# Values products behind the next scores, scores three units early, three output heads, last output step set apart

## The reference

```python
x = hidden_states                                # 1 x 1024 x 512, fp32
q = rope(x @ w_q); k = rope(x @ w_k); v = x @ w_v     # 32 query heads, 8 key/value heads, of 128
lq = x @ w_lq                                    # 1024 x 128
lk = rope(lq @ w_lk); lv = x @ w_lv              # 32 latent heads of 128
attn = causal_attn(q, k, v); lat = causal_attn(q, lk, lv)
x = layernorm(x + attn @ w_o + lat @ w_lo)
x = layernorm(x + top1_lora_experts(x))          # 8 experts of rank 16
```

## Time and profile before

| | |
|---|---|
| median of 3 runs | 2124.37 us (2123.72 to 2124.85) |
| the profiled execution | 2122.39 us |
| span of its profile, first to last instruction | 2120.6 us |
| busy: PE, DVE, ACT, POOL | 2026.5, 1409.2, 1044.6, 1060.2 us |
| granted TensorE clock, mean of the span | 0.994 of full speed |

### The profile page before, as it was taken

The page is one execution under the profiler, slowest core; times in us unless marked ns, Lnnn a source line. Parts: engine busy times, 40 slices in busy tenths (PEclk is TensorE's granted clock), DMA queues, the critical chain, the costliest instruction groups (busy, mean ns, idle before and its releaser), DMA issues.

```text
span 2120.6 us, 39951 instructions
## 1 busy us (share of the span) xinstructions
PE 2026.5 (96%) x12832; PEld 1824.3 (86%) x12832; DVE 1409.2 (66%) x3404; ACT 1044.6 (49%) x2461; POOL 1060.2 (50%) x873
## 2 busy tenths in 40 slices
PE   6999999999999999999999999999999999999995
PEld 5988889888898888988898898988989888898883
DVE  5757757576675757757577675767757576575766
ACT  3644626355363644626356373554626456273651
POOL 4536465364644537445364554536455364653630
PEclk9999999999999999999999999999999999999998
DMA  5010010100001000010100001010010100100001
GB/s 169 1 33 11 2 54 1 43 1 31 24 1 43 2 32 24 1 43 1 54 1 21 23 1 54 1 33 11 2 54 1 33 11 21 34 1 31 1 11 40
DMA packets 19367, 50.86 MB, mean 24 GB/s; under 512 B 5824, under 2 KB 7872, under 8 KB 19008
## 3 DMA queue, kind: packets, MB, share of 16 engines
q1 hardware_dynamic: 19136, 48.00, 6.8%
HBM read 45.89 MB, written 2.10 MB: 23 GB/s over the span
## 4 chain that ended last, share of the span: by engine, by line
PE 45%; issue 27%; POOL 24%; DVE 3%; POOLq 0%; ACT 0%; DVEq 0%; ACTq 0%
POOL probs L672 14%; PE ps L315 13%; PE ps L316 13%; PE ps L317 13%; PE ps L402 6%; POOL probs L663 4%; POOL ql_lo L667 4%; POOL pt_lo L648 1%; DVE pt_lo L679 1%; DVE stats L804 0%; POOLq L671 0%; PE ps L495 0%; PE ps L510 0%; POOL wlk_lo L654 0%; DVE probs L715 0%
## 5 line engine op out<-in xcount | busy, mean ns | idle before, releaser
L672 POOL TENSOR_TENSOR probs<-probs,inv_sum 128x640 f32<-128x640 f32 (+7 forms) x512 | 586.3, 1147 | 493.8 <-DVE inv_sum L746 493.1
L679 DVE TENSOR_TENSOR pt_lo<-ps,pt_hi 128x512 fp32r<-128x512 f32 (+3 forms) x768 | 401.6, 551 | 202.8 <-ACT pt_hi L517 199.6
L549 ACT ACTIVATE probs<-probs,neg_max 128x640 f32<-128x640 f32 (+7 forms) x512 | 397.6, 777 | 163.5 <-DVE neg_max L739 163.5
L517 ACT ACTIVATE pt_hi<-ps 128x512 fp32r<-128x512 f32 (+3 forms) x768 | 347.1, 486 | 185.3 <-PE ps L402 171.9
L739 DVE CUSTOM_DVE_ANT_0 probs<-ps,mask 128x640 f32<-128x640 f32 (+7 forms) x512 | 384.1, 753 | 57.6 <-PE ps L317 37.2
L315 PE MATMUL ps<-pt_hi,val_hi 128*128 128x256 f32 (+1 forms) x1280 | 371.0, 290 | 31.2 <-DVE pt_lo L679 31.2
L316 PE MATMUL ps<-pt_lo,val_hi 128*128 128x256 f32 (+1 forms) x1280 | 359.7, 281 | 0.0
L317 PE MATMUL ps<-pt_hi,val_lo 128*128 128x256 f32 (+1 forms) x1280 | 358.8, 280 | 0.0
L402 PE MATMUL ps<-ident,probs 128*128 128x128 f32 x2304 | 337.2, 274 | 15.4 <-POOL probs L672 13.3
L402 PEld LDWEIGHTS ps<-ident,probs 128*128 128x128 f32 x2304 | 266.1, 140 | 49.8 <-POOL probs L672 18.7
L315 PEld LDWEIGHTS ps<-pt_hi,val_hi 128*128 128x128 f32 x1280 | 242.5, 189 | 56.5 <-issue 55.0
(11 more groups left out here) (107 smaller groups left out, 4214.7 us busy)
## 6 DMA issues: line engine op xcount, KB each, us to landing
raw<-wo SPq DMA_DIRECT2D x32, 512.0 KB, 3.3
raw<-wq SPq DMA_DIRECT2D x16, 512.0 KB, 3.3
raw<-wlv SPq DMA_DIRECT2D x16, 512.0 KB, 3.9
raw<-wkv SPq DMA_DIRECT2D x8, 512.0 KB, 3.5
acc<-xT SPq DMA_DIRECT2D x4, 512.0 KB, 5.9
acc<-x SPq DMA_DIRECT2D x1, 2048.0 KB, 7.6
wlk_raw<-wlk SPq DMA_DIRECT2D x16, 128.0 KB, 4.0
out<-acc SPq DMA_DIRECT2D x8, 256.0 KB, 2.4
```

What stands on the lines that cost most here:

```text
L517: return nc.scalar.activation(dst, src, ACT.Copy)
L549: nc.scalar.activation(dst, dst, ACT.Exp, bias=neg_max[:, n % 8:n % 8 + 1], scale=-1.0, accum_out=row_sum[:, n % 8:n % 8 + 1]).then_inc(q[ ...
L672: nc.gpsimd.tensor_tensor(b, b, inv_sum[:, k % 8:k % 8 + 1].to_broadcast([P, b.shape[-1]]), ALU.mult).then_inc(q["normed"], 1)
L679: return nc.vector.tensor_tensor(dst, src, h, ALU.subtract)
```

## The change

Four edits, all of order; no operation is added or removed.

1. `UNITS`: q(1,0), q(1,1), lk(1,0) now follow one another, and v units that stood between them come later; the list ends with five v units, with v 2 and v 3 around lk(1,1).
2. `EARLY_UNIT = 3`: scores 0 and 1, their maxima and exponentials stand one unit earlier, before the last unit but two. Scores 2, and the reciprocals of 0 and 1, stay at the last unit.
3. The products of n = 2, 10, 18, 26 are no longer cut: the whole product stands behind the scores of slot n + 5. The product of n = 30 is also whole, in slot 35.
4. Outputs: the head of y = 2 moves from slot 34 to slot 33, ahead of turn_probs(30). Steps 0 and 1 of y = 0 and of y = 1 are done first, then step 3 of both, then y = 2, then the rest as before. The head's wait on the output weights is written in another place, for the same part.

```diff
--- before.py
+++ after.py
@@ -44,6 +44,7 @@
 O_BANKS = (6, 7)
 R_LAG = 3
 EARLY, MID = 2, 1
+EARLY_UNIT = 3
 T_LAG = 3
 LO_LAG = T_LAG + 1
 PV_LONG, PV_SHORT = 1, 3
@@ -64,14 +65,14 @@
 OUT_PARTS = (("ob", 0, 512, 1536), ("oa", 0, 1024, 0), ("ob", 512, 512, 1024))
 OUT_AFTER = (CHUNKS - 5, CHUNKS - 3, CHUNKS - 1)
 
-STEP_WEIGHTS = ((2, 0), (2, 512), (2, 1536), (3, 1024))
+STEP_WEIGHTS = ((2, 0), (2, 512), (1, 1536), (3, 1024))
 
 
 UNITS = (
-    [("q", 0, 0), ("q", 0, 1), ("k", 0, 0), ("k", 0, 1), ("lk", 0, 0), ("v", 0), ("lk", 0, 1), ("v", 1), ("q", 1, 0), ("v", 2),
-     ("q", 1, 1), ("v", 3), ("lk", 1, 0), ("v", 4), ("lk", 1, 1), ("v", 5), ("v", 6), ("v", 7)],
-    [("q", 0, 0), ("q", 0, 1), ("lk", 0, 0), ("v", 0), ("lk", 0, 1), ("v", 1), ("q", 1, 0), ("v", 2),
-     ("q", 1, 1), ("v", 3), ("lk", 1, 0), ("v", 4), ("lk", 1, 1), ("v", 5), ("v", 6), ("v", 7)],
+    [("q", 0, 0), ("q", 0, 1), ("k", 0, 0), ("k", 0, 1), ("lk", 0, 0), ("v", 0), ("lk", 0, 1), ("v", 1), ("q", 1, 0),
+     ("q", 1, 1), ("lk", 1, 0), ("v", 2), ("lk", 1, 1), ("v", 3), ("v", 4), ("v", 5), ("v", 6), ("v", 7)],
+    [("q", 0, 0), ("q", 0, 1), ("lk", 0, 0), ("v", 0), ("lk", 0, 1), ("v", 1), ("q", 1, 0),
+     ("q", 1, 1), ("lk", 1, 0), ("v", 2), ("lk", 1, 1), ("v", 3), ("v", 4), ("v", 5), ("v", 6), ("v", 7)],
 )
 ROPE_UNITS = tuple([u for u, x in enumerate(units) if x[0] != "v"] for units in UNITS)
 ROPES = tuple(len(x) for x in ROPE_UNITS)
@@ -84,7 +85,7 @@
 OUT_ORDER = tuple(2 * (ORDER[n] // 2) + x for n in (2, 3, 6, 7) for x in range(2))
 
 FIRST_STEP = 2
-HEAD = {TILES - 2 + T_LAG: (0, 1), TILES - 1 + T_LAG: (2,)}
+HEAD = {TILES - 2 + T_LAG: (0, 1, 2)}
 HEADS = sum(map(len, HEAD.values()))
 BANKS = 4
 
@@ -106,9 +107,7 @@
 for _n in range(2, TILES, 4):
     _blocks = blocks_of_product(_n)
     _k = _n + T_LAG + PV_LONG
-    _cut = _blocks // 2
-    PV_AFTER[_k] = (_n, 0, _cut)
-    PV_BEFORE[_k + 1] = (_n, _cut, _blocks)
+    PV_BEFORE[_k + 1] = (_n, 0, _blocks)
     O_SLOT[_k + 2] = _n
 for _n in range(3, TILES, 4):
     _k = _n + T_LAG + PV_SHORT
@@ -424,26 +423,24 @@
                 if j1 == last + 1:
                     mm.then_inc(q["pv_mm"], 1)
 
-            def outputs(g, pair, y, head=False):
+            def outputs(g, pair, y, steps):
                 t = OUT_ORDER[y]
-                begun = y < HEADS
-                if head:
+                if steps == (FIRST_STEP,):
                     pe.wait_ge(q["maxed"], per_pair(g, pair, TILES, TILES - (y < 2)))
-                    pe.wait_ge(q["wo_lo"], SEED + per_pair(g, pair, len(OUT_PARTS), 1))
                     pe.wait_ge(q["o_lo_made"], per_pair(g, pair, CHUNKS, (FIRST_STEP + 1) * ST // 2))
-                else:
+                if steps[-1] == STEPS - 1:
                     pe.wait_ge(q["o_lo_made"], per_pair(g, pair, CHUNKS, 3 * ST // 2 + y // 2 + 1))
                 if y >= 4:
                     pe.wait_ge(q["out_added"], SEED + per_pair(g, pair, ST, y - 3))
-                for step in (FIRST_STEP,) if head else (0, 1, 3) if begun else (2, 0, 1, 3):
+                for step in steps:
                     a, latent = divmod(step, 2)
                     lhs = [w[:, a, P * t:P * t + P] for w in ((ql_hi, ql_lo) if latent else (o_hi, o_lo))]
                     made, at = STEP_WEIGHTS[step]
-                    if y == 0 and not head:
+                    if y == 0:
                         pe.wait_ge(q["wo_lo"], SEED + per_pair(g, pair, len(OUT_PARTS), made))
                     mm = three(ps[:, y % 4, :], lhs, [w[:, 1, at:at + D] for w in (pt_hi, pt_lo)],
                                step == FIRST_STEP, step == STEPS - 1)
-                if not head:
+                if steps[-1] == STEPS - 1:
                     mm.then_inc(q["out_mm"], 1)
 
             pe.sem_inc(q["pv_mm"], SEED)
@@ -455,7 +452,7 @@
             with pe.Fori(0, GROUPS) as g:
                 for pair in range(PAIRS):
                     for u in range(len(UNITS[pair])):
-                        if u == len(UNITS[pair]) - 2:
+                        if u == len(UNITS[pair]) - EARLY_UNIT:
                             for n in range(EARLY):
                                 scores(g, pair, n)
                         if u == len(UNITS[pair]) - 1:
@@ -464,7 +461,7 @@
                         unit(g, pair, u)
                     for k in range(SLOTS):
                         for y in HEAD.get(k, ()):
-                            outputs(g, pair, y, head=True)
+                            outputs(g, pair, y, (FIRST_STEP,))
                         if EARLY + MID <= k < TILES:
                             scores(g, pair, k)
                         if k in PV_BEFORE:
@@ -473,8 +470,12 @@
                             turn_probs(g, pair, k - T_LAG)
                         if k in PV_AFTER:
                             with_values(g, pair, *PV_AFTER[k])
-                    for y in range(ST):
-                        outputs(g, pair, y)
+                    for steps in ((0, 1), (3,)):
+                        for y in range(2):
+                            outputs(g, pair, y, steps)
+                    outputs(g, pair, 2, (0, 1, 3))
+                    for y in range(HEADS, ST):
+                        outputs(g, pair, y, (2, 0, 1, 3))
 
 
             ra = raw[:, 0, 0:CT * (E + E * R)].rearrange("p (c n) -> p c n", c=CT)
@@ -766,7 +767,7 @@
                             values_lo(g, pair, u - 1)
                         if UNITS[pair][u][0] != "v":
                             rope(g, pair, ROPE_UNITS[pair].index(u))
-                        if u == last - 1:
+                        if u == len(UNITS[pair]) - EARLY_UNIT:
                             for n in range(EARLY):
                                 row_max(g, pair, n)
                         if u == last:
```

## The result

The changed kernel takes 2076.4 us (2075.5 to 2077.1 in 4 runs) against 2124.2 before: ratio 0.9775, 95% interval 0.976 to 0.979, 47.8 us faster. I forecast 2091, in a range from 2079 to 2105: right in direction, 14.6 us short in size, and 2.6 us outside the range.

A forecast was written before the change was run, and what follows sets the result against it. PE, busy 96% of the span, was taken as the bound, so only its idle time could be won. Pair 0 wins 1.57 us, pair 1 2.57, times 8 is 33 us: forecast 2091, range 2079 to 2105.

The forecast's parts named there:

- Edit 3: Products before PV(2), (10), (18), (26): 128-column scores of 0.28 us fill PE's wait, idle 0.31; 1.12 us a pass.
- (c): PE's stall before turn_probs(30), after the last matmul of the heads: 0.27 us lost.
- (d): PE's stall before step 3 of y = 0: 0.69 us where 0.23 would do, 0.46 lost.
- Edits 1 and 2 in pair 1: Projections and early scores of pair 1: normalization 0 and turn(0) come 1.0 us earlier, ends 0 to 1.7.
- The stall before v 4: Projections of pair 1: v 4 waits for its bank behind rope 6, a new stall of 0.3 to 0.4 us.
- The other leg: Pair 1, before normalization 0: reciprocals 2.05 us after v 6's end, at 698.55, later than rope 7's lo at 698.3.
- Third head: Around turn(30) and PV(30): 0.27 us won before the turn, 0.3 lost before PV(30); sum 0, ends -0.1 and +0.3.
- Last step apart: Outputs: steps 0, 1 of y = 1 cover the wait before step 3 of y = 0; 0.45 us a pass.
- The rule weighed in the prediction: About 81 ns per 128-column matmul, so 0.24 us for three and 15.6 us from edit 3 rather than 17.9.
- more is won: Rival, chance 0.08: pair 1's start stall goes wholly (0.7 more) and the third head keeps its 0.27; 2081 us.
- the start's stall in pair 1: PE's wait before turn_probs(0) in pair 1, 1.67 us; forecast to shrink by 1.0, in the rival to go wholly.
- No other: Other rivals: no gain in the order 0.16 (2099), product not hastened 0.05 (2109), slower 0.06 (2135), nothing 0.05 (2117 to 2124).

The follow-up runs named there:

- edit 3 on the other four: Kernel before, with only the products of n = 6, 14, 22 and 30 whole behind the scores, the others still cut: 2116.8 us, ratio 0.9957.

## Why the prediction was wrong, point by point

- **Edit 3** was the step that failed: "4 x 0.28 = 1.12 us a pass". Measured from PV(2) to turn(28) it is 1.76. Of the missing 0.64, 0.44 come from PV(6), (14), (22) (edit 3 on the other four gains 102.64 - 102.20 = 0.44 until turn(28)): I read the loop as cutting one product a step where it cuts two. The other 0.2 are size: each of the four wins (102.64 - 101.30) / 4 = 0.335, not 0.28. The 0.28 is the scores' own stretch, and they cost more than that where they stood: behind them the product's next matmul took 0.17 to its successor (603.17 to 603.34) for 0.12 elsewhere. PV(10) with the scores inside took 604.22 - 601.72 = 2.50 until the next transposes, the whole product takes 592.23 - 590.05 = 2.18, and it starts as long after turn_probs(11) as before (0.79 for 0.80). The row's idle 0.31 was not the length of the wait either. The transposes of turn_probs(11) alone need 0.24, so the wait was 0.56, and 0.27 of it is left; had it really been 0.31, no more than that could have been won. I had compared starts for the stalls (c) and (d), and not for this one. The mechanism itself (the end of the wait hangs on turn(8), 6.13 before, 6.11 after) held. Over 16 passes the step is 10 of the 14.6 us.
- **Edits 1 and 2 in pair 1**: 1.0 predicted, 1.30 measured. The stall before v 4 came (0.3 to 0.4 predicted; scores 3 start 0.46 later in the pass). The lo of rope 7 ended 27.7 us into the pass, 0.1 before the 27.8 counted. The other leg, the reciprocals at 2.05 behind v 6's end, did not: v 6 ends where scores 2 start, at 683.15, and they stand at 684.32, 1.17 behind it. The 2.05 held a wait for the exponentials, which had since moved ahead. So POOL started on tile 0 at the end of rope 7's lo, 1.5 us earlier in the pass. Pair 0 gained 0.18 where I said at most 0.1.
- **Third head**: 0 alone, right in mechanism and sum. In company I missed that edit 3 makes the wait before turn_probs(30) longer by 0.31 and that the head fills this as well. From turn(28) to the outputs the whole is -0.07 / -0.11 for the 0 predicted.
- **Last step apart**: 0.45 predicted, 0.54 / 0.56 alone. The wait's 0.46 was sized from starts; I left out that the matmul after a wait also takes longer to its successor, 652.00 to 652.33 against 0.23 elsewhere.
- **The sum**: products +0.64 / +0.65, start +0.18 / +0.30, outputs +0.13 / +0.15, tail -0.07 / -0.11, or 0.88 / 0.99 a pass, 15 us in all for the 14.6 missing. Every term but the last erred to the same side. The range allowed for a failed part, and on the side of more only for 12 us.
- **The rule weighed in the prediction** would have made the gain of edit 3 smaller still, 0.24 a product. The Trainium skill, "TensorE: Matmul & The Clock Gate", section "Back-to-back issue gap", gives about 81 ns for each matmul of 128 columns in a sustained stream. These traces have 0.28 or 0.29 us for the three, about 95 ns each, and 0.335 was won.
- **Rivals**: "more is won" came nearest (2081), but only in part by its path: the start's stall in pair 1 went, yet of the 1.36 by which turn_probs(0) came earlier 1.30 reached PV(2), and the third head kept its worth only beside edit 3. No other happened. That neither edit 1 nor edit 2 is good alone, and edit 2 harmful, was not in the text.
- **Signs in the profile after**: a step is 17.64 us, where 17.8 was said. The idle times before PV(10) and (18) are 0.02, but PV(26) of pair 0 keeps 0.39 (it had 0.68), and PV(2) of pair 0 has 0.40. PE is nowhere idle before step 3 or in the projections of pair 0. The waits of 0.27 before turn_probs(2) of pair 0 were not foreseen.

One thing stays open: why a matmul behind a wait or behind other operands takes 0.05 to 0.1 us longer to its successor, here seen and not explained.

## What to carry to other kernels

When a wait is to be filled, size it by the starts on either side against the same starts where nothing waits; the idle time in a row is only what is left of it, and a row without idle time can hide a wait of a quarter of a us. Size the work that is moved by what it costs where it stands, with the longer matmul behind it: 0.33 us here for a stretch of 0.28. Then list every place that the edit touches, from the loop's own numbers, and ask of each how near its operand comes: three places that looked free here were worth 0.14 us each.

An edit's worth belongs to its company. The third head went from -0.07 to +0.23 us a pass, and early scores from 13 us lost to a part of 11 won, because another edit had moved what stood before them in a queue; such edits are tried together and one by one.

## What the runs showed of the hardware

PE started 0.13 us after the end of the DVE write that it waited for, in each of three places read here (610.30, 592.85, 590.05). And a matmul's recorded end lay up to 0.25 us past the start of the next (a single transpose lasts 0.27 in its row and was followed after 0.03), which is how waits of 0.14 to 0.27 us before a product were missing from the idle times.

The first matmul behind a wait took longer to its successor: 0.33 for 0.23 with 512 columns (652.00 to 652.33), 0.22 for 0.12 with 256 (601.72 to 601.94).
